# Eight consecutive nodes on one partition in a two-layer graph kernel

## What is computed

```
sim   = tanh(adj * adj), kept where adj > 0        # and only the 350 largest of a row; rows here have fewer
h2    = tanh(x @ W_proj + b_proj)
x1    = layernorm(x + relu(sim @ (h2 @ W_gcn) + b_gcn))

pos   = (adj > 0) @ x1 ; neg = (adj < 0) @ x1      # neg is zero for these inputs
y     = [pos, neg] @ node_weight + node_bias * diag(adj)
      + (adj @ x1) @ edge_weight + edge_bias * diag(adj)
out   = layernorm(x1 + y)
```

## Time and profile before

| | |
|---|---|
| profiled execution | 610.62 us |
| its span | 608.8 us |
| TensorE busy | 600.5 us, 99% |
| VectorE busy | 471.2 us, 77% |
| ScalarE busy | 420.4 us, 69% |
| GpSimd busy | 187.7 us, 31%, in layer 0 only |
| moved | 130.67 MB, mean 215 GB/s |

### The profile page before, as it was taken

The page is one execution under the profiler, slowest core; times in us unless marked ns, Lnnn a source line. Parts: engine busy times, 40 slices in busy tenths (PEclk is TensorE's granted clock), DMA queues, the critical chain, the costliest instruction groups (busy, mean ns, idle before and its releaser), DMA issues.

```text
span 608.8 us, 5805 instructions
## 1 busy us (share of the span) xinstructions
PE 600.5 (99%) x1972; PEld 342.3 (56%) x1972; DVE 471.2 (77%) x690; ACT 420.4 (69%) x315; POOL 187.7 (31%) x88
## 2 busy tenths in 40 slices
PE   9999999999999999999999999999999999999996
PEld 6644444444444444555655656655665665657995
DVE  3767978888797979986497697697697697697843
ACT  3687686868768686558874865965865875865960
POOL 0598798887979697000000000000000000000000
PEclk9999999999999999999999999999999999999999
DMA  8999999999999991049787586586595685775000
GB/s 231 339 340 348 333 332 312 314 280 316 273 340 265 344 208 1 11 128 259 215 240 199 164 249 194 167 234 199 140 270 159 173 240 155 216 197 157 2 17 20
DMA packets 139455, 130.67 MB, mean 215 GB/s; under 512 B 9763, under 2 KB 139430, under 8 KB 139430
## 3 DMA queue, kind: packets, MB, share of 16 engines
q1 hardware_dynamic: 74390, 66.22, 39.3%
q10 hardware_dynamic: 65040, 64.17, 36.7%
HBM read 128.27 MB, written 2.10 MB: 214 GB/s over the span
## 4 chain that ended last, share of the span: by engine, by line
PE 92%; DMA 5%; DVE 1%; POOL 1%; ACT 1%; SPq 0%; issue 0%; DVEq 0%; ACTq 0%
PE acc L1059 34%; PE acc L1045 32%; PE stage L1068 10%; PE stage L1067 10%; DMA a_rows<-in_adj_dram 4%; PE stage L1059 2%; PE to_rows L1074 1%; PE to_rows L1073 1%; PE stage L1007 1%; PE to_rows L1024 1%; DMA x_rows<-in_x_dram 0%; POOL a_cols L390 0%; DVE a_cols L662 0%; ACT a_cols L593 0%; PE stage L1002 0%; POOL a_cols L384 0%
## 5 line engine op out<-in xcount | busy, mean ns | idle before, releaser
L662 DVE STREAM_TRANSPOSE a_cols<-a_rows 128x2048 f32<-128x2048 f32 x120 | 277.2, 2317 | 92.9 <-PE stage L1068 63.4
L1045 PE MATMUL acc<-a_cols,rhs 128*128 128x512 f32 x512 | 221.8, 593 | 1.8 <-ACT a_cols L593 1.1
L1059 PE MATMUL acc<-a_cols,x_rows 128*128 128x512 f32 (+1 forms) x512 | 212.3, 565 | 0.0
L1045 PEld LDWEIGHTS acc<-a_cols,rhs 128*128 128x128 f32 x512 | 96.4, 190 | 121.5 <-issue 117.8
L390 POOL TENSOR_TENSOR a_cols<-a_cols 128x1536 f32<-128x1536 f32 x56 | 153.2, 2747 | 35.0 <-DVE a_cols L662 34.6
L1059 PEld LDWEIGHTS acc<-a_cols,x_rows 128*128 128x128 f32 x512 | 96.6, 190 | 96.3 <-issue 92.4
L611 ACT ACTIVATE a_rows<-a_rows 128x4096 f32<-128x4096 f32 x32 | 116.1, 3627 | 46.2 <-DVE a_cols L662 38.1
L593 ACT ACTIVATE a_cols<-a_cols 128x2048 f32<-128x2048 f32 x56 | 107.1, 1912 | 49.8 <-POOL a_cols L390 49.2
L614 ACT ACTIVATE a_rows<-a_rows 128x4096 f32<-128x4096 f32 x32 | 115.9, 3621 | 1.0
L1067 PE MATMUL stage<-masks,x_hi 128*128 128x512 f32 (+1 forms) x288 | 115.0, 408 | 0.0
L1068 PE MATMUL stage<-masks,x_lo 128*128 128x512 f32 (+1 forms) x288 | 103.0, 366 | 0.0
(11 more groups left out here) (119 smaller groups left out, 271.5 us busy)
## 6 DMA issues: line engine op xcount, KB each, us to landing
a_rows<-in_adj_dram ACTq DMA_DIRECT2D x120, 512.0 KB, 10.4
a_rows<-in_adj_dram SPq DMA_DIRECT2D x120, 512.0 KB, 10.6
out_dram<-n_rows SPq DMA_DIRECT2D x28, 64.0 KB, 7.5
x_rows<-in_x_dram ACTq DMA_DIRECT2D x8, 64.0 KB, 2.5
x_rows<-in_x_dram SPq DMA_DIRECT2D x8, 64.0 KB, 2.4
x_rows<-in_x_dram ACTq DMA_DIRECT2D x4, 128.0 KB, 3.9
x_rows<-in_x_dram SPq DMA_DIRECT2D x4, 128.0 KB, 4.1
diag<-in_adj_dram SPq DMA_DIRECT2D x32, 0.5 KB
```

Source lines behind the costliest of these rows:

```text
L662: nc.vector.transpose(half_out(hs), half_in(s, h % HALVES)).then_inc(turned[layer], 1)
L1045: last = nc.tensor.matmul(acc[parity][:], rhs[:, b, :], a_cols[:, h % HSLOTS, k, :], start=(b == 0), stop=(b == BLOCKS - 1))
L1059: last = nc.tensor.matmul(sums, x_rows[:, b, :], rows(a_cols[:, h % HSLOTS, k, :]), start=(b == 0), stop=(b == BLOCKS - 1))
```

## The change

Eight consecutive nodes lie on one partition: node 1024 s + 8 p + b is on partition p, block b of span s. So

- x is loaded in runs of 2 and 4 KB, in 5 issues a queue where there were 12, each over 64 partitions.
- A turn reads every eighth word of a row (32 bytes apart), where it read every second (8 bytes). A half is blocks 0 to 3 or 4 to 7 of a span.
- A chunk is every eighth row of the whole matrix, chunk c of layer 0 being the rows 8 k + c. Each transfer still has 32 partitions x 16 rows x 1 KB.
- The results of a chunk need no reordering on the way: `z_t` and `sm_t` are copied straight.
- Stores and the diagonal go in one transfer where there were four and eight.
- The last rows of layer 0 are now block 7 of every span, in the second half of each piece. The first chunk of layer 1 leaves them out in halves 1 and 3 and makes them up behind half 3, and VectorE normalises them in one go behind half 3.

```diff
-    X_PARTS = [4, 4, 4, 4, 8, 8]
+    X_PARTS = [4, 4, 8, 8, 8]
+    QUEUE_HALF = [slice(0, P // 2), slice(P // 2, P)]
...
         def quarter_in(rows, s, q):
-            span, half = rows
-            src = adj[bass.ds(span * SPAN, SPAN), s * SPAN + q * PCOLS:s * SPAN + (q + 1) * PCOLS]
-            return src.rearrange("(r i h) k -> h i r k", h=2, i=SQ)[half]
+            src = adj[:, s * SPAN + q * PCOLS:s * SPAN + (q + 1) * PCOLS]
+            return src.rearrange("(r i b) k -> b i r k", b=PB, i=SQ)[rows]
...
+        def rows_out(rows):
+            return out.rearrange("(s p b) f -> b p s f", p=P, b=PB)[rows]
...
+            return x_rows[QUEUE_HALF[k], at:at + X_PARTS[part], :].rearrange("p b f -> p (b f)")
...
         def half_in(slot, h):
-            return a_rows[:, slot, :, :].rearrange("p r (m j e) -> p e r m j", j=SQ, e=2)[:, h]
+            return a_rows[:, slot, :, :].rearrange("p r (j b) -> p r b j", b=PB)[:, :, h * HB:(h + 1) * HB, :]
...
         def block_of(h, k):
-            return h // HALVES * PB + k * HALVES + h % HALVES
+            return h * HB + k
...
-                    for q in range(QUARTERS):
-                        for e in range(2):
-                            at = (span * SPAN + q * PCOLS + e) * (N + 1)
-                            sp.dma_start(diag[SQ * q:SQ * (q + 1), span * PB + e:(span + 1) * PB:2],
...
+                    sp.dma_start(diag[:, span * PB:(span + 1) * PB],
+                                 bass.AP(adj.tensor, span * SPAN * (N + 1), [[PB * (N + 1), P], [N + 1, PB]]))\
...
-                for q in range(QUARTERS):
-                    sp.dma_start(rows_out(rows, q),
-                                 n_rows[SQ * q:SQ * (q + 1), parity, :, :]).then_inc(stored[parity], 16)
+                sp.dma_start(rows_out(rows), n_rows[:, parity, :, :]).then_inc(stored[parity], 16)
...
-                for q in SP_QUARTERS:
-                    sp.dma_start(rows_out(rows_of(1, LAST), q)[:, at:at + tiles, :],
...
+                sp.dma_start(rows_out(rows_of(1, LAST))[QUEUE_HALF[0], at:at + tiles, :],
...
-                nc.scalar.activation(by_tile(z_t[:]), by_set(acc[parity][:]), ACT.Relu, bias=b_col[:, 1:2])\
+                nc.scalar.activation(z_t[:], acc[parity][:], ACT.Relu, bias=b_col[:, 1:2])\
...
-                        if h in (3, 4, 5):
-                            norm0(LAST, h - 3)
+                        if h == HSLOTS - 1:
+                            for part in range(3):
+                                norm0(LAST, part)
...
             def first_chunk():
-                for h in range(HPC):
-                    if h == 0:
-                        pe.wait_ge(lo_ready, CHUNKS - 1)
-                    if h == HPC - HALVES:
-                        pe.wait_ge(lo_ready, CHUNKS)
+                waiting = [h for h in range(HSLOTS) if h % HALVES]
+                pe.wait_ge(lo_ready, CHUNKS - 1)
+                for h in range(HSLOTS):
                     pe.wait_ge(masked, h + 1)
-                    with_adj(acc[0][:], h, all_rows)
+                    ready = range(HB - 1) if h in waiting else range(HB)
+                    with_adj(acc[0][:], h, all_rows, ready)
...
+                pe.wait_ge(lo_ready, CHUNKS)
+                for h in waiting:
+                    with_adj(acc[0][:], h, all_rows, [HB - 1])
+
+                    with_masks(acc_m[0][:], h, all_rows, [HB - 1]).then_inc(half_used[1], 1 if h == 1 else 2)
+                for h in range(HSLOTS, HPC):
+                    pe.wait_ge(masked, h + 1)
+                    with_adj(acc[0][:], h, all_rows)
+                    with_masks(acc_m[0][:], h, all_rows).then_inc(half_used[1], 1)
```

More of the change, by code:

```diff
@@ L189, in rows_at, with diag_at @@
         def rows_at(t, rows):
[L190 to L201, removed]
+            return t.rearrange("p (s b) f -> p b s f", b=PB)[:, rows]
+        def diag_at(rows, s):
+            return diag[:, s * PB + rows:s * PB + rows + 1]
         def part_of(cols, at, tiles):
-            return cols.rearrange("p (q m i) -> p q m i", q=QUARTERS, i=SQ)[:, :, at:at + tiles, :]\
-                .rearrange("p q m i -> p q (m i)")
+            return cols[:, at * P:(at + tiles) * P]
         feat_t = early[:, 0, :]
@@ L312, in rows_of @@
         def rows_of(layer, chunk):
-            return (chunk[1] * -1 + (PIECES - 1), 1 - chunk[2]) if layer else (chunk[1], chunk[2])
+            return CHUNKS - 1 - chunk[0] if layer else chunk[0]
         def next_of(chunk):
-            c, span, parity = chunk
-            return c + 1, span + parity, 1 - parity
+            return chunk[0] + 1, None, 1 - chunk[2]
         def is_first(c):
@@ L496, in _, with load_x @@
         def _(act):
[L497 to L499 removed]
+            def load_x(part):
+                act.dma_start(x_of(part, 1), x_in(part, 1)).then_inc(x_loaded[part], 16)
             def load_quarter(rows, s, q):
@@ L622, in keep_sums @@
                 act.wait_ge(half_used[1], HPC * (c + 1))
-                nc.scalar.copy(by_tile(z_t[:]), by_set(acc[parity][:])).then_inc(sums_kept, 1)
+                nc.scalar.copy(z_t[:], acc[parity][:]).then_inc(sums_kept, 1)
             each_chunk(layer1)
@@ L630, in _ @@
                 act.wait_ge(last_summed, part + 1)
-                nc.scalar.copy(by_tile(z_t[:])[:, :, at:at + tiles, :],
-                               last_acc[part][:, 0:tiles * P].rearrange("f (q m i) -> f q m i", q=QUARTERS, i=SQ))\
-                    .then_inc(sums_kept, 1)
+                nc.scalar.copy(part_of(z_t, at, tiles), last_acc[part][:, 0:tiles * P]).then_inc(sums_kept, 1)
                 act.wait_ge(ln_step, LN_STEPS * (2 * CHUNKS - 1 + part) + 2)
@@ L929, in g_block @@
                         nc.vector.tensor_tensor(g_sum, g_sum, stage[1][:, 0:F], ALU.add).then_inc(g_added, 1)
-                    with dve.Fori(0, PIECES) as s, dve.Fori(0, TILES) as m:
-                        for e in range(2):
-                            g_block(u * BLOCKS + s * PB + m * 2 + e, s, m, e)
+                    with dve.Fori(0, PIECES) as s, dve.Fori(0, PB) as b:
+                        g_block(u * BLOCKS + s * PB + b, s, b)
                     dve.wait_ge(g_added, (u + 1) * (BLOCKS + 1))
@@ L1034, in layer0 @@
                     if not before:
-                        for g in range(h // HALVES * HALVES, h // HALVES * HALVES + 2):
-                            emptied(pe, USES.index(("rhs", g)))
+                        emptied(pe, USES.index(("rhs", h)))
                     if before:
@@ L1054, in all_rows, with with_adj @@
                 return cols
-            def with_adj(sums, h, rows):
-                for k in range(HB):
+            def with_adj(sums, h, rows, part=range(HB)):
+                for k in part:
                     b = block_of(h, k)
@@ L1061, in with_adj, with with_masks @@
                 return last
-            def with_masks(sums_m, h, rows):
-                for k in range(HB):
+            def with_masks(sums_m, h, rows, part=range(HB)):
+                for k in part:
                     b = block_of(h, k)
```

79 lines of the change are left out of this document (33 added, 46 removed).

## The result

The changed kernel takes 719.46 us (median of 6 runs, 717.01 to 724.09), the kernel before 609.68 beside it: a ratio of 1.1806 [1.1762, 1.1849], 18% slower. The prediction was 607.8 us with a range up to 700; the time lies outside both. What happened is its first rival, to which it gave a chance of 0.38: VectorE became the bound.

What follows compares the result with a forecast made beforehand. TensorE was taken as the bound, working 600.5 of 608.8 us. Gains of 1.1 + 0.4 (its two waits) + 0 + 0.3 (last store) = 1.8 us gave 607.8 us against the median 609.61; range 605.5 to 700.

Steps and rivals of the forecast that it cites:

- first rival: VectorE's turns at twice the time for an element, 4.52 us, make VectorE the bound: 770 us together; chance 0.38.
- The turn's read pattern: VectorE's turn reading every eighth word instead of every second: no change from 2317 ns a turn, priced at 0.
- The point of decision: Layer 0: VectorE has 4.6 us left a chunk, 0.57 a turn, so it becomes the bound from 2.89 us a turn.
- Layer 1: VectorE's load in its chunks if turns slow: 33.5 + 17.6 = 51.1 us against 43.8, 7.3 eight times, 58 us.
- x, priced at 0: Loading x at the start in larger transfers (128 KB a queue, not two of 64): 0, ends 0.3 either way.
- The two waits: TensorE's waits of 1.1 us (near 52 us) and 0.7 us (first tanh): earlier adj gains 1.1 and 0.4 us.
- The last store: End of the kernel, one issue less a queue: 0.3 us gained, ends 0.4 gained and 0.6 lost.
- Eighth rows: Chunks of adj made of every eighth row: price 0 if transfers stay near 347 GB/s; layer 0 needs 301.
- first chunk of layer 1: Left-out blocks made up behind the fourth half, norm moved to one place: slack 8 us, price 0.
- copies: The contiguous z_t and sm_t copies keep their size; no cost was put on them.
- the transfer rival: Row pitch slows adj's loads until transfers bound layer 0: 641 us, or 629 by the skill's ratio; chance 0.10.
- The range: Whole kernel: 605.5 to 700 us, past the transfer rival and VectorE's milder half, leaving out turns at twice their time.

Runs made afterwards that it cites:

- experiment 1: The changed kernel with VectorE's turn reading every second word again, as in the kernel before: 612.07 us, ratio 1.0029.
- Experiments 4 to 8 and 12: Changed kernel, turn reading at steps 4, 1, 3, 7, then word pairs, then single words, both 32 bytes apart: 719.05, 610.26, 628.29, 724.57, 618.74, 719.78 us.
- experiment 3: The changed kernel with the eighth-word read in layer 0's turns only and the second-word read in layer 1's: 676.16 us, ratio 1.1083.
- experiment 10: The changed kernel with VectorE's copy of the mask sums placed one turn earlier in layer 1's chunks: 712.84 us, ratio 1.168.
- experiment 5: The changed kernel with VectorE's turn reading neighbouring words (step 1): 610.26 us, one run.
- experiment 9: experiment 1 with the first two parts of x cut again into two 64 KB transfers a queue, over 32 partitions each: 610.38 us, ratio 1.0007.
- experiment 11: The kernel before with only its parts of x changed, to 4, 4, 8, 8, 8 blocks from 4, 4, 4, 4, 8, 8: 611.57 us, ratio 1.0015.

## Why the prediction was wrong, point by point

- **The turn's read pattern, priced at 0: this step failed, and with it all.** Measured, it cost 1.61 us for each of the 120 long turns and 0.80 for each of the 16 short ones, and with VectorE as the bound 107 us of the 110 (experiment 1). The text took the row at a step of two as the nearest to a step of eight, with the argument that a step of two "already skips half of what it passes". Experiments 4 to 8 and 12 show what was wrong with that: skipping is not what is paid for. A step of two still finds a second wanted word in the same 16 bytes, a step of four or eight does not. Two forms of a rule stood in the prediction. The softer one in the Trainium skill (SBUF — State Buffer, note on cachelines) asks for at least two hits in each 16 bytes; the prediction quoted it and weighed it too lightly, and all eight patterns agree with it. The strict form in the Trainium skill (Vector Engine (DVE) Microarchitecture Reference, "Measured stream behaviour on trn2") lets only runs of two or more adjacent words go at full rate; the 2319 ns of step 2 refute it here. Its 1.73 ns for a source that hops at every element is near the 1.87 measured here. To drop it for being wrong at step 2 was to lose its figure for step 8.
- **The point of decision held.** Above 2.89 us a turn layer 0 pays. Put into the rival's own sum, 3.93 us gives 23.3 + 8 x 1.61 = 36.2 us for a chunk; 35.9 was measured, and experiment 3 puts layer 0 at 64.1 us in all.
- **Layer 1 was undersized.** The same sum gives 33.5 + 12.9 = 46.4 us, 2.6 more a chunk, some 21 us; it cost 43.3. First, 33.5 was too low: it is the mean of two windows that don't begin at the same place of a chunk, and from one weighing to the next VectorE was busy for 34.4 us before (first row of experiment 10). That gives 34.4 + 12.9 = 47.3, as measured, and 3.5 us a chunk, 28 in all. Second, the sum took VectorE's busy time for its whole need, but the gaps between its instructions add about 0.7 (47.3 busy of 48.0, experiment 10). Third, the two engines wait for each other over the copied sums, about 1 us a chunk. Together some 5.2 us, and a chunk took 49.0 in the mean where it took 43.8; eight chunks make 42 of the 43.3 us. The third has a price of its own in the changed kernel, here TensorE behind the wait (start us, us, what, idle before):

```profile
515.47 0.70 PE L1046 MATMUL to_rows<-w_pne,z_t 128*128 128x128 f32 x2 [3.09 <-issue]
515.96 0.64 PE L1047 MATMUL to_rows<-w_pne,sm_t 128*128 128x128 f32 x2
516.39 0.63 PE L1046 MATMUL to_rows<-w_pne,z_t 128*128 128x128 f32 x2
```

  The pairs follow each other in 0.43 us. In experiment 10, where nothing is waited for there, they do so in 0.22:

```profile
511.09 0.38 PE L1046 MATMUL to_rows<-w_pne,z_t 128*128 128x128 f32 x2
511.31 0.39 PE L1047 MATMUL to_rows<-w_pne,sm_t 128*128 128x128 f32 x2
```

  Short windows of the changed kernel show why (columns as in the earlier trace rows):

```profile
514.00:515.40 1.40, 0.00 (x0) 0.00 (x0) 1.40 (x3) 1.40 (x1) 0.00 (x0) 1.00 0.00 0
515.40:516.40 1.00, 0.93 (x5) 0.94 (x6) 1.00 (x1) 0.43 (x2) 0.00 (x0) 0.60 0.00 0
516.40:517.40 1.00, 1.00 (x6) 1.00 (x6) 1.00 (x1) 0.00 (x0) 0.00 (x0) 0.50 0.39 92
519.50:521.00 1.50, 1.50 (x8) 1.25 (x7) 0.89 (x1) 1.50 (x1) 0.00 (x0) 1.00 1.13 300
```

  TensorE had stood still for 3.09 us; then the granted clock fell to 0.50 of full speed, its lower level of 1.2 GHz, and it was back at 1.00 (2.4 GHz) from 519.5 us on, TensorE having worked without a gap. In experiment 10 it was 1.00 from 511.0 to 512.8 us, where the same products ran without a wait. The eight pairs took 3.3 us in place of 1.7, and VectorE's next turn waited 0.70 us for TensorE. Not every wait does this: in layer 0 from 158.06 to 193.94 TensorE stands still four times for the tanh, 6.0 us in all and 2.8 at the longest, and the granted clock is 1.00.
- **x, priced at 0 with ends of 0.3: failed.** In experiment 1 the second part of x came so late (5.25 us after its issue, not 2.89) that TensorE waited 2.0 us. The size of the transfers points to part of it (experiment 9), the larger parts behind them perhaps to the rest (experiment 11); neither share is resolved. Adj started at 5.03 us and not 4.0, because an issue took 0.56 to 0.62 us and not 0.47; what sets that time is open.
- **The two waits, 1.1 and 0.4 gained: gone, but the gain is shown for neither in full.** In experiment 1 TensorE comes 2.2 us later to both, which hides them by itself. In experiment 5 it comes only 0.6 later (24.43 us), and both are gone, so some 0.5 us of the 1.1 at least came from the earlier adj. The 0.4 did not come: the first long tanh began at 22.98 us there, behind ACT's own work, and at 22.64 before.
- **The last store, 0.3 gained: wrong in sign.** In experiment 1 VectorE's last write is at 606.91 and the span ends at 610.3, 3.4 us later; before it was 605.80 and 608.8, 3.0 later. All eleven traces with the new store have 3.4 to 3.5, the three with the old one 3.0, 3.0 and 3.7. So one larger transfer costs about 0.4 more than an issue saved; it lies within the ends given (0.4 gained, 0.6 lost).
- **Eighth rows, first chunk of layer 1, copies: right.** 347 to 351 GB/s at full traffic, 27.90 us a chunk in experiment 1, and no wait of TensorE behind the start in it. (In the working of the first chunk 258 + 2.3 + 1.2 is 261.5 and not 261.7, which changes nothing.) The row of the Trainium skill from which the transfer rival took its 629 us (DMA: Bandwidth & Descriptors, HBM row pitch) gives the pitch from one partition's row to the next partition's. Here that pitch is 32 KB before and 128 KB now, while the 1 and 4 MB are distances between rows of one partition. So that estimate compared unlike things, and the runs neither confirm nor refute the row.
- **The range.** It held half of the VectorE rival on purpose and ended at 700. With a turn at 3.93 us the rival's sum would have given 8.3 x 7 + 8 + 21 = 87 us, and about 697 in all: it was layer 1 that put the time outside.

No version here beats the kernel before clear of noise. In this turn consecutive words of one read go to consecutive partitions, so to have four or eight consecutive nodes on one partition the read must step by four words or more, which costs VectorE's lead. The savings at the head and the tail that came along with the change did not pay by themselves: 1.0029, 1.0007 (not told from 1) and 1.0015 in experiments 1, 9 and 11.

## What to carry to other kernels

A new access pattern needs a price of its own: ask not how far apart its words are but how many of each 16 bytes it uses, since VectorE ran at 1.08 ns an element with two or more and at 1.87 with one, and multiply the difference by every instruction that has it before calling it nothing. Where no row shows the pattern and one answer is nothing and the other 100 us, the chance of the dear one follows from rules that speak for it, not from the nearest row, whose nearness is itself the assumption. Fewer and larger transfers at the head are no sure gain when an early product waits for one of them: time the landing, in more than one trace, and not the issues saved. And where an engine becomes the bound, count its need from one fixed point of a chunk to the next.

## What had not been expected of the hardware

- The stair of the steps: 2304, 2319, 3085, 3940, 3937, 3931 ns for steps of 1, 2, 3, 4, 7, 8 words, and 2305 for pairs 32 bytes apart.
- TensorE ran at half pace in some early stretches and not in others. Behind a wait for x the same products took nearly twice as long in experiment 1 as in experiment 5, whose head is the same (start us, us, what, idle before), first experiment 1, then 5:

```profile
7.33 1.12 PE L976 MATMUL stage<-ident,x_rows 128*128 128x128 f32 x4 [2.02 <-DMA x_rows<-in_x_dram]
8.24 1.91 PE L981 MATMUL stage<-early,w_pg 128*128 128x512 f32 x2
```
```profile
7.30 0.66 PE L977 MATMUL stage<-ident,x_rows 128*128 128x128 f32 x4 [2.05 <-DMA x_rows<-in_x_dram]
7.80 1.02 PE L982 MATMUL stage<-early,w_pg 128*128 128x512 f32 x2
```

  The length of the wait does not decide it: experiments 3 and 9 had the slow products (1.91 us) behind 0.8 us. It can cost nearly as much as the wait: with equal waits the first product of layer 0 began at 26.00 in one and 24.43 us in the other. The windows there give a granted clock of 1.00 in both; what slowed the products is open.
- TensorE stood still for 3.09 us at a granted clock of 1.00, and then ran at 0.50 (windows above).
- The same issue took different times in different company: that of `w_pg` 0.42 us between loads of x over 32 partitions, 0.56 between loads over 64.
